# Auxiliary work in six places of a score unit instead of three, with the low part of the probabilities multiplied last

## The reference, cut to what matters

```python
x = x + tanh(g_xattn[0]) * xattn(layernorm(x), ctx, w_q, w_k, w_v, w_o, b_o)   # softmax over 1444 keys
x = x + tanh(g_ffn[0]) * ffn(layernorm(x), ...)
# ffn: X = X + attn(rmsnorm(X)) @ wo;  h2 = rmsnorm(X)
#      combine = softmax of the two best of softmax(h2 @ router_w)
#      return X + swiglu_shared(h2) + sum_e combine[:, e] * swiglu_e(h2)
```

## Time and profile before

| what | value |
|---|---|
| time, median of 3 runs (lowest to highest) | 1496.37 us (1490.59 to 1496.73) |
| the profiled execution's own time, and its span | 1497.34 us, 1495.6 us |
| PE busy | 1362.4 us, 91% |
| DVE busy | 1058.8 us, 71% |
| ACT busy | 809.3 us, 54% |
| POOL busy | 589.5 us, 39% |
| mean granted clock of PE | 0.975 of 2.4 GHz |

### The profile page before, as it was taken

One profiled execution on the slowest core, in us unless ns is written; L12 is line 12 of the kernel. 1 busy time (PEld: TensorE's weight loads), 2 busy tenths in 40 slices (PEclk: granted clock), 3 DMA queues, 4 the chain that ended last, 5 costly groups with the idle time before them and its releaser, 6 DMA issues.

```text
span 1495.6 us, 23587 instructions
## 1 busy us (share of the span) xinstructions
PE 1362.4 (91%) x8776; PEld 826.5 (55%) x8776; DVE 1058.8 (71%) x1996; ACT 809.3 (54%) x1188; POOL 589.5 (39%) x702
## 2 busy tenths in 40 slices
PE   4759999999999999999999999999999999788898
PEld 4235555555656565655555555555555555456676
DVE  2677677767686767676777777777777775866765
ACT  1034656555655655555556565656565655554654
POOL 3023334343443444443444343434343433453554
PEclk9589999999999999999999999999999999999999
DMA  7020202020201001020202020202020100000000
GB/s 218 29 57 1 58 1 58 1 58 1 58 1 37 23 21 38 2 57 1 58 1 58 1 58 1 58 1 58 1 57 2 43 1 1 1 1 2 7 7 11
DMA packets 66934, 42.86 MB, mean 29 GB/s; under 512 B 52966, under 2 KB 62410, under 8 KB 66826
## 3 DMA queue, kind: packets, MB, share of 16 engines
q1 hardware_dynamic: 66826, 41.43, 10.7%
HBM read 15.38 MB, written 0.82 MB: 11 GB/s over the span
## 4 chain that ended last, share of the span: by engine, by line
PE 66%; DVE 14%; POOL 9%; issue 4%; ACT 4%; DMA 2%; SPq 0%; DVEq 0%; POOLq 0%; ACTq 0%
PE psum L755 19%; PE psum L815 8%; PE psum L736 7%; PE psum L738 7%; PE psum L740 7%; DVE mx L1239 4%; POOL p_lo L431 4%; PE psum L768 4%; PE psum L855 3%; PE psum L807 3%; PE psum L842 3%; PE psum L781 3%; PE psum L864 2%; DVE p_lo L431 2%; DVE y_sb L1261 2%
## 5 line engine op out<-in xcount | busy, mean ns | idle before, releaser
L950 ACT ACTIVATE p<-psum 128x800 f32<-128x800 f32 x384 | 320.9, 836 | 522.9 <-PE psum L740 521.0
L1239 DVE TENSOR_REDUCE mx<-psum 128x1 f32<-128x512 f32 (+1 forms) x624 | 385.8, 653 | 63.4 <-PE psum L815 58.0
L431 POOL TENSOR_TENSOR p_lo<-p,p_hi 128x800 f16<-128x800 f32 x128 | 243.9, 1906 | 468.3 <-ACT p_hi L951 461.8
L755 PE MATMUL psum<-p_hi,c_both 128*128 128x400 f16 x1536 | 389.3, 335 | 25.0 <-POOL p_lo L431 14.3
L951 ACT ACTIVATE p_hi<-psum 128x800 f16<-128x800 f32 x384 | 319.3, 831 | 0.0
L815 PE MATMUL psum<-cT_both,qk_hi 96*128 96x512 f16 (+1 forms) x624 | 231.1, 387 | 54.5 <-DVE y_sb L1261 16.4
L431 DVE TENSOR_TENSOR p_lo<-p,p_hi 128x800 f16<-128x800 f32 x256 | 259.4, 1013 | 21.4 <-ACT p_hi L951 18.9
L755 PEld LDWEIGHTS psum<-p_hi,c_both 128*128 128x128 f16 x1536 | 146.7, 98 | 145.5 <-issue 33.7
L736 PE MATMUL psum<-qk_hi,cT_both 97*128 97x400 f16 x768 | 195.5, 335 | 2.9 <-DMA qk_hi<-mrow 2.9
L755 PE MATMUL psum<-p_lo,c_both 128*128 128x400 f16 x768 | 194.6, 335 | 0.0
L738 PE MATMUL psum<-qk_lo,cT_both 96*128 96x400 f16 x768 | 194.5, 334 | 0.0
(11 more groups left out here) (183 smaller groups left out, 1795.7 us busy)
## 6 DMA issues: line engine op xcount, KB each, us to landing
c_both<-c_new SPq DMA_DIRECT2D x16, 768.0 KB, 4.9
ctx_nat<-in_ctx_dram SPq DMA_DIRECT2D x16, 528.0 KB
wg<-in_L_ffn_e_gate_dram SPq DMA_DIRECT2D x1, 1024.0 KB, 5.5
wu<-in_L_ffn_e_up_dram SPq DMA_DIRECT2D x1, 1024.0 KB, 7.5
wd<-in_L_ffn_e_down_dram SPq DMA_DIRECT2D x8, 128.0 KB, 4.9
out_dram<-x SPq DMA_DIRECT2D x4, 200.0 KB
x<-in_x_dram SPq DMA_DIRECT2D x1, 600.0 KB
p<-in_L_xattn_w_q_dram SPq DMA_DIRECT2D x1, 512.0 KB, 4.1
```

Of the source, the lines that this page charges most:

```text
L431: engine.tensor_tensor(p_lo[0:m, i % 3, :, :], p32[0:m, i % 3, :, :], p_hi[0:m, i % 3, :, :], ALU.subtract).then_inc(lo_made(b, i)[0], 1)
L755: t = mm(outs[k], w[parity][0:m, j, :], p[0:m, i % 3, k, :], start=(j == 0 and w is c_hi and p is p_hi), stop=(j == CH - 1 and w is c_lo))
L950: a(p32[0:m, i % 3, :, :], src, ACT.Exp, scale=DH ** -0.5)
L1239: v.tensor_reduce(mx[:, rt, part:part + 1], bank[:, 0:w], AX.X, ALU.max)\
```

## The change

`slots_of` puts the auxiliary units of a score unit in six places in place of three. All that are not maxima go to places 2 and above (one: place 2; two: 2 and 4; three: 2, 3, 4; four: 2, 3, 4, 5). The maxima go where there are fewest units so far, the lowest place first. On PE the places are: 0 after the first pass of the scores, 1 after the second, 2 after the third, 3 and 4 after the first and second pass of `pv_unit`, 5 after its last. On DVE places 0 and 1 come before `probs_rest`, the rest after it (and after `split_weights` in the last batch). In `pv_unit` the pass with `p_lo` is now the last, and the wait for `p_lo` stands right before it. The order in which the auxiliary units take banks changes with the lists.

```diff
+    def slots_of(units):
+        slots = [[] for _ in range(6)]
+        maxima = [u for u in units if u[0] == "p"]
+        others = [u for u in units if u[0] != "p"]
+        for n, u in enumerate(others):
+            slots[2 + 4 * n // len(others)].append(u)
+        for u, k in zip(maxima, sorted(sorted(range(6), key=lambda k: (len(slots[k]), k))[0:len(maxima)])):
+            slots[k].append(u)
+        return slots
...
-        thirds = [[us[len(us) * k // 3:len(us) * (k + 1) // 3] for k in range(3)] for us in by_place]
-        return thirds, at
+        return [slots_of(us) for us in by_place], at
...
                 for k in range(2):
                     mm(outs[k], cT_hi[parity][:, cols], qk_hi[parity][:, qs[k]], start=True, stop=False)
+                between(0)
                 for k in range(2):
                     mm(outs[k], cT_hi[parity][0:C, cols], qk_lo[parity][:, qs[k]], start=False, stop=False)
+                between(1)
...
-                pe.wait_ge(*lo_made(b, i))
...
-                for w, p in ((c_hi, p_hi), (c_hi, p_lo), (c_lo, p_hi)):
+                for n, (w, p) in enumerate(((c_hi, p_hi), (c_lo, p_hi), (c_hi, p_lo))):
+                    if p is p_lo:
+                        pe.wait_ge(*lo_made(b, i))
...
-                    if w is c_hi and p is p_hi:
-                        between()
+                    if n < 2:
+                        between(3 + n)
...
-                    one, two, three = steps(kind)[0][i]
-                    run_aux(aux, one, b, kind, parity)
+                    slots = steps(kind)[0][i]
+                    for slot in slots[0:2]:
+                        run_aux(aux, slot, b, kind, parity)
                     if i and i - 1 not in LO_POOL:
                         probs_rest(dve, v, b, i - 1)
...
-                    run_aux(aux, two, b, kind, parity)
                     if kind == "last" and 0 <= i - 4 < 3 * NW_PARTS:
...
                         split_weights(*divmod(i - 4, NW_PARTS))
-                    run_aux(aux, three, b, kind, parity)
+                    for slot in slots[2:]:
+                        run_aux(aux, slot, b, kind, parity)
```

More of the change, by code:

```diff
@@ L155, in numbered @@
         return at
+    def slots_of(units):
[7 more added lines that the diff above has]
+        return slots
     def steps(kind):
         kinds = {"first": KINDS_FIRST, "last": KINDS_LAST}.get(kind, KINDS_MID)
-        by_place = [[u for u in plan[i] if u[0] in kinds] for i in range(UNITS)]
+        by_place = [[u for slot in slots_of([u for u in plan[i] if u[0] in kinds]) for u in slot] for i in range(UNITS)]
         at = numbered([u for us in by_place for u in us])
-        thirds = [[us[len(us) * k // 3:len(us) * (k + 1) // 3] for k in range(3)] for us in by_place]
-        return thirds, at
+        return [slots_of(us) for us in by_place], at
     def aux_base(b, kind):
@@ L719, in _, with score_unit @@
             set_wait(pe, set_pool, SET_POOL, "head_mask")
-            def score_unit(b, parity, i):
+            def score_unit(b, parity, i, between):
                 g, j = divmod(i, CH)
@@ L741, in score_unit, with pv_unit @@
                 t.then_inc(scores, 1)
-            def pv_unit(b, parity, i, between=lambda: None):
+            def pv_unit(b, parity, i, between=lambda n: None):
                 j = i % CH
                 m = kc(j)[1]
-                pe.wait_ge(*lo_made(b, i))
                 if i == 0:
@@ L752, in pv_unit @@
                 outs = [psum[:, ACCB + k, 0:GW] for k in range(2)]
-                for w, p in ((c_hi, p_hi), (c_hi, p_lo), (c_lo, p_hi)):
+                for n, (w, p) in enumerate(((c_hi, p_hi), (c_lo, p_hi), (c_hi, p_lo))):
+                    if p is p_lo:
+                        pe.wait_ge(*lo_made(b, i))
                     for k in range(2):
                         t = mm(outs[k], w[parity][0:m, j, :], p[0:m, i % 3, k, :],
-                               start=(j == 0 and w is c_hi and p is p_hi), stop=(j == CH - 1 and w is c_lo))
-                    if w is c_hi and p is p_hi:
-                        between()
+                               start=(j == 0 and n == 0), stop=(j == CH - 1 and p is p_lo))
+                    if n < 2:
+                        between(3 + n)
                 t.then_inc(pv, 1)
@@ L880, in body, with between @@
                 for i in range(UNITS):
-                    score_unit(b, parity, i)
-                    one, two, three = steps(kind)[0][i]
-                    run_aux(aux, one, b, kind, parity)
-                    def middle():
-                        run_aux(aux, two, b, kind, parity)
+                    slots = steps(kind)[0][i]
+                    def between(n):
+                        run_aux(aux, slots[n], b, kind, parity)
+                    score_unit(b, parity, i, between)
+                    between(2)
                     if i >= 2:
-                        pv_unit(b, parity, i - 2, middle)
+                        pv_unit(b, parity, i - 2, between)
                     elif kind != "first":
-                        pv_unit(b - 1, 1 - parity, UNITS - 2 + i, middle)
+                        pv_unit(b - 1, 1 - parity, UNITS - 2 + i, between)
                     else:
-                        middle()
-                    run_aux(aux, three, b, kind, parity)
+                        between(3)
+                        between(4)
+                    between(5)
             batches(pe, body)
             for i in (UNITS - 2, UNITS - 1):
+                pe.wait_ge(probs_hi, (B - 1) * UNITS + (i + 1))
                 pv_unit(B - 1, 1, i)
@@ L1010, in body @@
                         act.wait_ge(scores, b * UNITS)
-                    for third in steps(kind)[0][i]:
-                        run_aux(aux, third, b, kind, parity)
+                    for slot in steps(kind)[0][i]:
+                        run_aux(aux, slot, b, kind, parity)
                     if i == 1 and kind != "first":
```

## The result

| | before | after |
|---|---|---|
| median of the runs, us | 1495.78 (4 runs, 1490.59 to 1496.73) | 1516.45 (4 runs, 1515.48 to 1519.48) |
| profiled execution's span, us | 1495.6 | 1517.7 |
| one middle batch, us | 77.70 (mean of 13) | 79.53 (mean of 13) |

The changed kernel takes 1.016 times as long, 95% interval 1.014 to 1.018. The prediction was 1468 us and faster: the sign is wrong, and the time lies above the range too.

The account below looks back on a forecast made before the run. PE's list was taken to set the pace, with 6.5 us of late starts in a 77.8 us middle batch; 1.75 us gained in each of 14 batches (24.5) and 4 at both ends gave 1468 us, 8-in-10 range 1449 to 1498.

Parts of the forecast that it names:

- the rival "lock": Units 6 to 8: later norm_1 makes POOL's two p_lo run back to back, f0 late 4.5 us; 1505 us, chance 0.07.
- The sentence on the rule: DVE and POOL share a port pair: DVE's p_lo of unit 7 would wait for POOL, possibly xf too.
- The term of 1.9 us: PE's stop at f0 in unit 8, waiting for hn: 1.9 us in place of 0.95 in each middle batch.
- The clock rival: The stop at f0 halves PE's clock for about 5 us, costing 2.4; 1502 us if in each batch, chance 0.10.
- the bunches of units 11 and 19: Maxima standing third or fourth in a bunch lose their wait in each middle batch, 0.8 us.
- the waits of f11 and f13 for y0's heads: Units 15 and 17: f11 waits 0.15 us for 0.4 before, f13 0.6 for 0.65.
- the starts late by less than 0.25 us: Small late starts of PE over a middle batch, claimed to fall from 1.1 to 0.3 us.
- 71.3 us of work: PE's own work in a middle batch of 77.8 us, which the change leaves as it is.
- the 0.77 us for POOL's p_lo: PE's stop for POOL's p_lo of unit 6 in each of 14 middle batches, 10.8 us together.
- "Swallowed": Rival: DVE limits more than units 4 to 9, half or all of the 24.5 us lost; 1481 to 1496, chance 0.12.
- The ends of the program: First and last batch: 4 us of gain together, bounds -2 and 8.

Follow-up runs that it names:

- POOL waits: The changed kernel, but POOL's p_lo of unit 8 begins only when hn is made: 1472.28 us, ratio 0.986 to the kernel before.
- the places alone: The six places with the old order of passes and the old wait for p_lo: 1520.77 us, ratio 1.017 to the kernel before.
- p_lo first: The kernel before, but in middle batches DVE makes p_lo of unit 7 ahead of xf and hn: 1555.41 us, ratio 1.041.
- the last run: Changed kernel with xf, hn and ln's statistics earlier on DVE, f0 behind unit 8's last pass, and a batch's first maximum one pass later: 1451.87 us, 0.970.
- ln early: Changed kernel with xf and hn before p_lo of unit 7, f0 behind unit 8's last pass, ln's statistics before p_lo of unit 5: 1452.67 us, 0.972.
- the filler: The changed kernel with twelve extra matmuls of 400 columns, result overwritten, before PE's wait for hn at f0: 1494.32 us, ratio 0.999.

## Why the prediction was wrong

By its own steps, in the batch that the rows show, with the start of unit 4's scores as 0:

| step of the prediction | forecast | measured |
|---|---|---|
| unit 4's first maximum waits | no | no (734.55) |
| ln's statistics done | 8.9 | 9.1 |
| first step of norm_1 takes | 0.22 | 0.22 |
| unit 8 begins | 11.1 | 11.3 |
| POOL's p_lo of unit 6 | 11.8 to 13.5 | 12.0 to 13.7 |
| DVE's p_lo of unit 7 ends | 14.3 | 14.5 |
| **xf and hn end** | **14.95** | **16.5** |
| stop at f0 | 1.9 | 3.2 |
| granted clock after it | 1.00 | 0.50 for 3.4 us |
| a plain middle batch | 75.95 | 79.05 |

**The step that failed** is "That p_lo can start at 13.0, but POOL's p_lo of unit 6 runs from 11.8 to 13.5 [...] DVE's ends at 14.3, xf and hn at 14.95." All of it held up to the word hn. I had applied the lock to the p_lo of DVE and not to the two short steps behind it. The number needed stood further on, in the rival "lock": POOL's p_lo of unit 8 is ready at 14.3, and by the sum hn was to start at about 14.6, behind it. So hn had to wait for POOL's whole step. The sentence on the rule even names such a case ("and xf too if POOL started its next one in between"), but it was not carried into the sum. The term of 1.9 us was 3.17 in this batch and 3.08 in most. And the last batch of the kernel before, from which the rule was read, showed that such short steps of DVE wait too (xf 1.82 us, hn 1.73).

**The clock rival came true**, at a chance of 0.10. Its price was 2.4 us a batch; measured, it is 1.71, 24 us in 14 batches. What I held against it was that 0.95 us at 733.94 left the clock alone, which says nothing of a stop two or three times as long. The two faults are linked: with a stop of 1.50 us in the brackets (POOL waits) the clock stays, with 2.92 to 3.00 it falls. Whether it would have stayed at the forecast stop of 1.9 alone no run shows. The nearest rows speak against it: 1.88 at 108.23 was followed by half clock in the first batch, 2.0 behind 0.7 was in 12 of 14 batches with the places alone, and 2.44 behind 0.65 in 13 of 14 with p_lo first. So 0.10 was too little even by the forecast's own stop.

**The lock rival** had the right mechanism and the wrong place. POOL's two p_lo did not run back to back (0.89 us of idle time between them), norm_1 ended at 11.8 for 11.6, and so what it priced did not happen; hn lost 1.4 us to the second of them all the same.

**The rest of the sum was right in total, and in part by luck.** A plain batch stands 3.10 us over the forecast; the stop explains 1.2 of it and the clock 1.71. With the lock taken out, the kernel takes 1472.28 us for a forecast of 1468 and a plain batch 75.99 for 75.95. No stop for POOL's p_lo remains in a middle batch, the bunches of units 11 and 19 flow, and maxima inside the scores start without loss where their bank is free. But the single terms don't all hold. f0's stop was 1.66 there for 1.9, and the waits of f11 and f13 for y0's heads (0.15 and 0.6 forecast) don't occur in middle batches: PE stops at L877 for y_sb once in the whole changed kernel. Against that stand the starts late by less than 0.25 us, forecast at 0.8 with those of units 1 and 2. By the prediction's own 71.3 us of work they are some 1.9 (an estimate: 75.99 less 71.3, less 1.66 at f0, 0.32 at f2 and 0.83 in unit 13). One reading was off as well: the 0.77 us for POOL's p_lo is that of the batch read, and 12 of the other 13 show 0.65, so that stop was worth about 0.1 us less. "Swallowed" is refuted: with the late starts gone DVE is no limit, and the total of a period fell as reckoned.

**The ends of the program** were priced at a gain of 4 us. Up to the first f0 the changed kernel is 4.0 us later (194.60 against 190.58), and behind the last of the 13 periods it is 5.6 us quicker: 1.6 in all. In the first batch PE waits 11.41 us for the transposed context, where it waited 9.84, as the prediction had named. One execution of each can't test this term, though. With POOL waiting all lists but for this one wait are the same up to this f0, the wait is 11.13 us, and f0 comes at 189.19, 5.4 us earlier. 1.4 of these are its shorter stop; behind most of the others stands the clock, which was granted at 0.54 and 0.50 from 114 to 116 and from 148 to 150 us in the changed kernel's execution and at 1.00 in the other.

**Missed altogether**: the transposed context now comes late in middle batches too, in every third (0.38 to 0.58 us).

```profile
94.43 0.59 PE L828 MATMUL psum<-cT_both,qk_hi 96*128 96x512 f16 x1 [11.41 <-DMA cT_both<-c_new]
...
416.63 0.38 PE L828 MATMUL psum<-cT_both,qk_hi 96*128 96x512 f16 x1 [0.42 <-DMA cT_both<-c_new]
...
655.48 0.38 PE L828 MATMUL psum<-cT_both,qk_hi 96*128 96x512 f16 x1 [0.53 <-DMA cT_both<-c_new]
```

With POOL waiting these batches are longer than their neighbours by 0.7 us, which is this stop. In the changed kernel three of the four are longer by some 1.6 us, and about 1.0 of that is the clock and not the DMA: after f0 at 590.91, 829.87 and 1068.50 it was granted at 0.50 for over 6 us, and already the stop at L873, some 19 us behind f0, comes 1.0 us later. The period from 194.60 is as long (80.23 us) with such a long stretch at half clock and no late context. The maxima that read the new context stand ahead of the place at which they stood, which used up their cover: placed one pass later (the last run) three batches had the stop instead of five. Why it is each third batch no run settles; with "ln early" and with the filler it comes at other distances too.

## What to carry to other kernels

When a step of DVE is moved, lay it and every step behind it against POOL's list at the new time, the short ones above all: what such a step costs is not its length but what is left of POOL's step, unless it leads POOL by more than a tenth of a microsecond. A stop of PE that grows has a second price, which comes all at once: read from the trace which stops it came through at full clock in every batch (here up to 1.62 us), and give the clock a large chance where the forecast stop is beyond the longest of these. The limit isn't sharp: one stop of 2.0 us can keep the clock and the same stop lose it in the next batch. Spreading the auxiliary units was worth what the count of late starts said; the order of three steps on DVE decided whether it came to 1516 or 1464 us, so look at the engine that feeds the moved unit before the engine that runs it.

## What the runs showed of the hardware

- **Which of DVE and POOL goes first is decided by a tenth of a microsecond, and below that the starts of the rows don't tell it.** xf, whose row starts 0.12 us ahead of POOL's (748.69 and 748.81), took 0.34 us, as it did 0.10 us ahead with the filler; hn, 0.14 us behind it (748.95), waited to POOL's end and took 1.72. But with p_lo first in the kernel before, hn's row starts 0.05 to 0.06 us ahead of POOL's in 12 of 14 batches, and hn still waits 1.5 us, as xf does in the last batch of the kernel before, 0.05 us ahead (1279.39 and 1279.44). Each xf and hn that waited ends some 0.08 us after POOL's step. For xf and hn beside a p_lo of POOL no lead between 0.06 and 0.10 us occurs in these runs, so the boundary isn't known more closely.

```profile
843.26 1.83 DVE L1182 TENSOR_SCALAR hn<-x,aggr,ps 100x128 f32<-100x128 f32 x1
...
843.32 1.70 POOL L431 TENSOR_TENSOR p_lo<-p,p_hi 128x800 f16<-128x800 f32 x1 [1.08 <-ACT p_hi L951]
```

- **Reduces of maxima, which read PSUM, kept their length beside POOL** (1.25 us for two at 746.27).
- **Stops and the clock.** Stops of 2.9 to 3.0 us in the changed kernel were followed by a granted clock of 0.50 in all 14 batches, stops of 2.3 to 2.4 behind one of 0.65 to 0.77 in 13 of 14, stops of 2.0 behind 0.72 to 0.85 in 12 of 14; stops of 1.50 to 1.62 us left it at 1.00 in all. Matmuls whose result nobody reads, put into the stop, kept it at 1.00 and were worth 1.71 us a batch, though f0 was as late as ever.
